# A language-model layer on one core: the state-space kernel for four channels per partition, with longer rows and weight columns further apart

## The reference, cut to what matters

```
h  = adaptive embedding(ids) * 16                    # gather of 384 values, times a 384 x 256 matrix
xn = layernorm(h)
x1 = xn @ w1.T + b                                   # 256 channels
xc = silu(depthwise conv of x1, 3 taps)
y[b, t, c] = D[c] * xc[b, t, c] + sum over u <= t of  K[c, t - u] * xc[b, u, c]
             with K[c, n] = sum over 16 states s of B[c, s] * C[c, s] * sigmoid(A[c, s]) ** n
h  = h + (y * silu(xn @ v1.T + b)) @ w2.T + b
h  = h + (shared gated MLP + mean of 2 hashed experts)(layernorm(h)) / 2
```

## Time and profile before

| | us |
|---|---|
| median of three runs | 439.96 |
| the profiled execution, its time | 440.18 |
| its span, first to last instruction | 438.3 |
| phase A, until the first matmul with Toeplitz weights | 130.2 |
| state-space matmuls | 130.2 to 157.6 |
| first expert matmul | 175.5 |

### The profile page before, as it was taken

One profiled execution on the slowest core, in us unless ns is written; L12 is line 12 of the kernel. 1 busy time (PEld: TensorE's weight loads), 2 busy tenths in 40 slices (PEclk: granted clock), 3 DMA queues, 4 the chain that ended last, 5 costly groups with the idle time before them and its releaser, 6 DMA issues.

```text
span 438.3 us, 8454 instructions
## 1 busy us (share of the span) xinstructions
PE 399.5 (91%) x2880; PEld 351.6 (80%) x2880; DVE 272.8 (62%) x607; ACT 243.5 (56%) x435; POOL 211.5 (48%) x236
## 2 busy tenths in 40 slices
PE   3869999899998874999999999999999999998996
PEld 2858788788677863788898988988988888897885
DVE  6667998889756778464565565564554654655333
ACT  4567777768887436635535635635635536435442
POOL 6578988831005555648337247247247336433000
PEclk9999999999999989899999999999999999999999
DMA  2424111249699982101111211201301301100101
GB/s 63 145 80 161 49 58 57 65 129 323 182 312 303 239 314 96 50 0 49 53 45 48 59 40 49 84 11 48 96 0 49 96 0 49 48 0 0 49 0 48
DMA packets 32779, 38.86 MB, mean 89 GB/s; under 512 B 3461, under 2 KB 29027, under 8 KB 32624
## 3 DMA queue, kind: packets, MB, share of 16 engines
q1 hardware_dynamic: 29616, 32.99, 24.3%
q0 software_dynamic: 3136, 5.52, 4.1%
HBM read 34.56 MB, written 8.65 MB: 99 GB/s over the span
## 4 chain that ended last, share of the span: by engine, by line
PE 65%; DVE 15%; POOL 6%; ACT 6%; issue 4%; DMA 3%; DVEq 0%; SPq 0%; ACTq 0%; POOLq 0%
PE ps L1152 20%; PE ps L1153 20%; PE ps L1154 20%; DVE hid_lo L1085 3%; DMA h_in<-h_rows_dram 2%; DVE stat L963 2%; POOL bias_e L657 1%; POOL bias_e L658 1%; PE ps L1160 1%; PE ps L1271 1%; PE ps L1190 1%; DVE x_mid L1016 1%; DVE act_out L1079 1%; ACT act_out L857 1%; DVE catT_lo L956 1%
## 5 line engine op out<-in xcount | busy, mean ns | idle before, releaser
L1085 DVE SCALAR_TENSOR_TENSOR hid_lo<-act_out,hid_hi 128x512 fp32r<-128x512 f32 x64 | 54.4, 851 | 57.6 <-ACT hid_hi L870 57.6
L857 ACT ACTIVATE act_out<-ps,vec 128x512 f32<-128x512 f32 x32 | 22.0, 689 | 90.5 <-PE ps L1154 90.5
L1079 DVE SCALAR_TENSOR_TENSOR act_out<-ps,vec,act_out 128x512 f32<-128x512 f32 x32 | 24.0, 751 | 55.6 <-ACT act_out L857 55.6
L687 POOL TENSOR_TENSOR h_sb<-h_sb,bias_e 128x256 f32<-128x256 f32 x32 | 24.5, 769 | 53.6 <-DVE h2n L976 53.6
L1154 PE MATMUL ps<-h2nT_hi,sw_lo 128*128 128x512 f32 x128 | 50.0, 391 | 0.0
L1153 PE MATMUL ps<-h2nT_lo,sw_hi 128*128 128x512 f32 x128 | 50.0, 391 | 0.0
L1152 PE MATMUL ps<-h2nT_hi,sw_hi 128*128 128x512 f32 x128 | 49.9, 390 | 0.0
L680 POOL TENSOR_TENSOR zc_lo<-v_sb,zc_hi 128x256 fp32r<-128x256 f32 x32 | 28.9, 907 | 34.4 <-ACT zc_hi L847 34.4
L861 ACT ACTIVATE act_out<-ps,vec 128x512 f32<-128x512 f32 x32 | 22.1, 689 | 40.4 <-PE ps L1154 40.3
L537 POOL DMA_INDIRECT cat<-table_dram,x_ids x32 | 35.7, 1115 | 8.4 <-issue 5.8
L870 ACT ACTIVATE hid_hi<-act_out 128x512 fp32r<-128x512 f32 x64 | 39.7, 622 | 0.0
(11 more groups left out here) (133 smaller groups left out, 1254.2 us busy)
## 6 DMA issues: line engine op xcount, KB each, us to landing
toep_l<-kernel_rows_dram SPq DMA_DIRECT2D x14, 512.0 KB, 9.0
toep_r<-kernel_rows_dram SPq DMA_DIRECT2D x12, 512.0 KB, 6.4
h_rows_dram<-h_ring SPq DMA_DIRECT2D x32, 128.0 KB, 1.8
h_in<-h_rows_dram SPq DMA_DIRECT2D x8, 512.0 KB, 4.5
stage<-w_e_dram POOLq DMA_DIRECT2D x7, 512.0 KB, 3.6
out_dram<-o_sb SPq DMA_DIRECT2D x7, 512.0 KB, 3.2
bias_e<-rows_dram SPq DMA_DIRECT2D x1, 1024.0 KB, 7.3
toep_r<-kernel_rows_dram SPq DMA_DIRECT2D x4, 256.0 KB, 7.7
```

The costliest lines, as they stand in the source:

```text
L687: nc.gpsimd.tensor_tensor(at, at, bias_e[:, bass.ds(e, 1), :].rearrange("p o c -> p (o c)"), ALU.add).then_inc(h2_biased, 1)
L857: nc.scalar.activation(act_out[:, n % 4, :], ps[bank][:, :], ACT.Silu, bias=vec[:, C_SB1 + j:C_SB1 + j + 1]).then_inc(act_done, 1)
L1079: nc.vector.scalar_tensor_tensor(act_out[:, n % 4, :], ps[bank + 1][:, :], vec[:, C_SB3 + j:C_SB3 + j + 1], act_out[:, n % 4, :], ALU.add, ...
L1085: nc.vector.scalar_tensor_tensor(hid_lo[:, n % 4, :], act_out[:, n % 4, :], 0.5 if kind == SHARED else 0.25, f32(hid_hi[:, n % 4, :]), ALU ...
```

## The change: what it does

- Rows in DRAM are for four channels: 16 bytes per position. A Toeplitz tile is [128, 4 groups, 128 lags, 4 channels, high/low], so its runs are 2 KB (1 KB in the half parts that were 512 bytes) and there are half as many. The same weights lie 8 f16 apart instead of 4, 16 bytes.
- Each partition computes K for four channels (64 states) and 64 lags: partitions 0 to 63 lags 0 to 63, partitions 64 to 127 lags 64 to 127, whose first value is multiplied with the decay to the power 64. The parameters come by two loads of their own (`k_par`), issued ahead of the weights; `vec` is loaded after them.
- DVE squares six times, forms the first values (two linked products) and doubles up to 16 lags per state, the last on 1024 elements after the fourth embedding split; the two products for `mid_bias` move there. POOL does one doubling in 8 steps, then 14 fold steps and the last sum, the D, the split: 26 steps instead of 30. The row is stored by two DMAs.
- The zeros in front of each row are copied once from the zeroed `x_pad` to DRAM by SP, and the memset of `k_row` goes. ACT waits for that copy before phase A, which writes `x_pad`.

```diff
-    toep_r = sb(ssm_mem, "toep_r", [P, TRIGHT, PAIRS, SEQ, 2, 2], F16, R)
+    toep_r = sb(ssm_mem, "toep_r", [P, TRIGHT, QUADS, SEQ, WIDE, 2], F16, R)
...
-    power = flat[:, 0:HALVES * STATES * SEQ].rearrange("p (s t) -> p s t", t=SEQ)
+    power = flat[:, 0:WIDE * STATES * HALF].rearrange("p (s t) -> p s t", t=HALF)
...
@@ SP
         sp.dma_start(x_ids[:, :, :], ids.rearrange("(g p r) -> p g r", p=P, r=RES)).then_inc(ids_in, 16)
+        for h in range(2):
+            params = bass.AP(small.tensor, C_A, [[2 * NSMALL, NQUAD], [NSMALL, 2], [1, NK]])
+            sp.dma_start(k_par[h * NQUAD:(h + 1) * NQUAD, :, :], params).then_inc(k_par_in, 16)
+        sp.dma_start(raw_a[:, 0:KC * D], w_a[:, 0:KC * D]).then_inc(wa_in, 16)
         sp.dma_start(vec[:, :], small).then_inc(vec_in, 16)
-        sp.dma_start(raw_a[:, 0:KC * D], w_a[:, 0:KC * D]).then_inc(wa_in, 16)
+        sp.wait_ge(pad_zero, 1)
+        sp.dma_start(bass.AP(kernel_rows.tensor, 0, [[YLEN * WIDE, NQUAD], [1, (SEQ - 1) * WIDE]]),
+                     x_pad[0:NQUAD, :, :, :].rearrange("p a b t -> p (a b t)")[:, 0:(SEQ - 1) * WIDE]).then_inc(rows_zero, 16)
...
-            src = bass.AP(kernel_rows.tensor, q * PAIRS * 2 * YLEN + 2 * (h * HALF + t),
-                          [[2, HALF], [2 * YLEN, PAIRS], [1, 2 * (SEQ - t)]])
+            src = bass.AP(kernel_rows.tensor, q * QUADS * WIDE * YLEN + WIDE * (h * HALF + t),
+                          [[WIDE, HALF], [WIDE * YLEN, QUADS], [1, WIDE * (SEQ - t)]])
...
@@ POOL, kernel_step
-            if n < 4:
+            if n < 8:
                 double(5, 8 * n, 8)
-            elif n < 12:
-                double(6, 4 * (n - 4), 4)
+            elif n < 16:
+                c, part = (n - 8) // 2, (n - 8) % 2
+                fold((slice(c, c + 1), slice(4 * part, 4 * part + 4)), 8)
...
+                for h in range(2):
+                    lags = bass.AP(kernel_rows.tensor, (SEQ - 1 + h * HALF) * WIDE, [[YLEN * WIDE, NQUAD], [1, HALF * WIDE]])
+                    row = k_row[h * NQUAD:(h + 1) * NQUAD, :, :, :].rearrange("p t c w -> p (t c w)").bitcast(F32)
+                    pool.dma_start(lags, row).then_inc(k_out, 16)
...
@@ DVE
-        double(0)
-        double(1)
+        for k in range(6):
+            square(k)
+        first = power[:, :, 0].rearrange("p (i s) -> p i s", i=2)
+        link(nc.vector.tensor_tensor(first, k_par[:, :, K_B:K_C], k_par[:, :, K_C:K_D], ALU.mult))
+        later = power[NQUAD:P, :, 0]
+        link(nc.vector.tensor_tensor(later, later, abar[NQUAD:P, 6, :], ALU.mult))
...
-        beside_cat = {0: lambda: double(2), 1: lambda: double(3), 2: lambda: double(4), 3: last_square}
+        beside_cat = {0: two_doubles, 1: lambda: double(2), 2: lambda: double(3), 3: last_double}
...
@@ PE
-                t_hi, t_lo = toep(q)[:, j // 2, :, j % 2, 0], toep(q)[:, j // 2, :, j % 2, 1]
+                t_hi, t_lo = [toep(q)[:, j // WIDE, :, j % WIDE, w] for w in range(2)]
```

More of the change, by code:

```diff
@@ L44 @@
 YLEN = 256
-PAIRS = CH // 2
+WIDE = 4
+QUADS = CH // WIDE
+NQUAD = D // WIDE
 HALF = SEQ // 2
 C_W1B, C_V1B, C_CONV = 0, 2, 4
-C_A, C_B, C_C, C_D = 10, 42, 74, 106
+C_A = 10
+K_A, K_B, K_C, K_D, NK = 0, 32, 64, 96, 98
 C_SB1, C_SB3, C_B1 = 108, 112, 116
@@ L564, in double, with fold @@
             k_link(nc.gpsimd.tensor_tensor(power[:, at, n:2 * n], power[:, at, 0:n], by, ALU.mult))
[L566 to L570, removed]
+        by_channel = power[:, :, :].rearrange("p (c s) t -> p c s t", c=WIDE)
+        def fold(at, keep):
+            by_s = by_channel[:, at[0], :, :]
+            first = by_s[:, :, at[1], :]
+            second = by_s[:, :, at[1].start + keep:at[1].stop + keep, :]
+            k_link(nc.gpsimd.tensor_tensor(first, first, second, ALU.add))
+        K_STEPS = 26
         def kernel_step(n):
-            halves = power[:, :, :].rearrange("p (h s) t -> p h s t", h=HALVES)
-            row_hi, row_lo = [k_row[:, SEQ - 1:2 * SEQ - 1, :, w].rearrange("p t c -> p c t") for w in range(2)]
+            row_hi, row_lo = [k_row[:, :, :, w].rearrange("p t c -> p c t") for w in range(2)]
+            if n >= K_STEPS:
+                return
             if n == 0:
@@ L579, in kernel_step @@
                 pool.wait_ge(k_pool, k_steps)
-            if n < 4:
+            if n < 8:
                 double(5, 8 * n, 8)
-            elif n < 12:
-                double(6, 4 * (n - 4), 4)
+            elif n < 16:
+                c, part = (n - 8) // 2, (n - 8) % 2
+                fold((slice(c, c + 1), slice(4 * part, 4 * part + 4)), 8)
             elif n < 20:
[L585 to L595, removed]
+                fold((slice(n - 16, n - 15), slice(0, 4)), 4)
+            elif n < 22:
+                fold((slice(2 * (n - 20), 2 * (n - 20) + 2), slice(0, 2)), 2)
+            elif n == 22:
+                k_link(nc.gpsimd.tensor_tensor(k_sum[:, :, :], by_channel[:, :, 0, :], by_channel[:, :, 1, :], ALU.add))
+            elif n == 23:
+                first = k_sum[0:NQUAD, :, 0].rearrange("p (i c) -> p i c", i=2)
+                k_link(nc.gpsimd.tensor_tensor(first, first, k_par[0:NQUAD, :, K_D:NK], ALU.add))
+            elif n == 24:
                 k_link(nc.gpsimd.tensor_copy(row_hi, k_sum[:, :, :]))
@@ L753, in _ @@
     def _(act):
-        act.wait_ge(vec_in, 16)
-        nc.scalar.activation(abar[:, 0, :], vec[:, C_A:C_A + 32], ACT.Sigmoid).then_inc(abar_done, 1)
+        act.wait_ge(k_par_in, 32)
+        nc.scalar.activation(abar[:, 0, :].rearrange("p (i s) -> p i s", i=2), k_par[:, :, K_A:K_B], ACT.Sigmoid).then_inc(abar_done, 1)
         act.wait_ge(half_set, 1)
@@ L921, in _ @@
         nc.vector.scalar_tensor_tensor(all_mask, all_ids, 0.0, all_mask, ALU.is_ge, ALU.mult).then_inc(mask_step, 1)
[L922 to L927, removed]
         dve.wait_ge(abar_done, 1)
@@ L936, in double @@
             n = 1 << k
-            by = abar[:, k, :].rearrange("p (s o) -> p s o", o=1).broadcast_to([P, HALVES * STATES, n])
+            by = abar[:, k, :].rearrange("p (s o) -> p s o", o=1).broadcast_to([P, WIDE * STATES, n])
             link(nc.vector.tensor_tensor(power[:, :, n:2 * n], power[:, :, 0:n], by, ALU.mult))
+        for k in range(6):
             square(k)
-        def last_square():
-            square(5)
-            assert steps == K_FIRST
-        double(0)
-        double(1)
+        first = power[:, :, 0].rearrange("p (i s) -> p i s", i=2)
+        link(nc.vector.tensor_tensor(first, k_par[:, :, K_B:K_C], k_par[:, :, K_C:K_D], ALU.mult))
+        later = power[NQUAD:P, :, 0]
+        link(nc.vector.tensor_tensor(later, later, abar[NQUAD:P, 6, :], ALU.mult))
         dve.wait_ge(wa_hi, 1)
@@ L950, in _, with two_doubles, last_double @@
                                 f32(proj_hi[:, :, :].rearrange("p k n -> p (k n)")), ALU.subtract).then_inc(wa_lo, 1)
-        beside_cat = {0: lambda: double(2), 1: lambda: double(3), 2: lambda: double(4), 3: last_square}
+        def two_doubles():
+            double(0)
+            double(1)
+        def last_double():
+            dve.wait_ge(vec_in, 16)
+            for half in range(HALVES):
+                nc.vector.tensor_tensor(mid_bias[:, half:half + 1], vec[:, C_W1B + half:C_W1B + half + 1],
+                                        vec[:, C_CONV + 3 * half + 1:C_CONV + 3 * half + 2], ALU.mult)
+            double(4)
+            assert steps == K_FIRST
+        beside_cat = {0: two_doubles, 1: lambda: double(2), 2: lambda: double(3), 3: last_double}
         def cat_lo(i, r):
```

25 lines of the change are left out of this document (13 added, 12 removed).

## The result

The changed kernel took 449.43 us (median of four runs, 448.91 to 450.69); the kernel before, on the same chip, 439.95 (four runs, 439.21 to 440.4). The ratio is 1.0217, 95% interval 1.0199 to 1.0235: 2.2% slower. The forecast was 449.7. The profiled execution took 449.91 us with a span of 448.0, 9.7 more than before.

The account below looks back on a forecast made before the run. PE, busy 91%, bounds the kernel, except where it waits for the first mixer output, set by POOL's chain. Weight step 8.7 plus late start 1.0 on 440.18 us gave 449.9, 0.2 less for timed runs: 449.7; range 438.3 to 451.3.

Parts of the forecast that it names:

- The weight step: State-space matmuls: weights 16 bytes apart double spacing from 33.3 to 66.7 ns; first mixer output 8.7 us later.
- the loads stay at full pace: Rival for state-space matmuls: weight loads do not feel the 16-byte step; 439.0 us; chance 0.40.
- a part of the price: Rival for state-space matmuls: spacing only 50 to 62 ns; at 60 ns, 446.3 us; chance 0.10.
- The turns between the tiles: PE's seven output turns between Toeplitz tiles, four transposes each, at 0.47 us: 3.3 us of the stage.
- The late start: Kernel's front: moved DVE doubling steps delay the first normalization and ACT's hn by 1.0 us (0 to 1.4).
- The idle time that I counted against it: DVE before L963 at 16.33 us: 0.4 us idle, to absorb part of the 1.2 us of added doubling work.
- parts 3 and 4: DVE's moved doubling steps (+1.0 us, early squares 0); POOL's reduced work, zeroing copy and extra parameter load and store (0).
- part 2: Toeplitz loads at 116 to 158 us: longer runs gain 0 to 5 us, taken as 2, worth nothing if weights slow.
- POOL's chain: Before the first mixer output: bias row, second h_in, expert weight splits, zc_lo; last before, no longer last after the change.
- 1.77 us of room: At the first mixer output: the PE chain ended 1.77 us before POOL's, so that much matmul delay costs nothing.
- a plain shift: From first mixer output to first expert matmul and the end: the same steps run, so output delay passes on unchanged.
- the first rival: Weight loads keep full pace despite 16-byte steps: 439.0 us, 435.3 at best; chance 0.40.

Follow-up runs that it names:

- experiment 1: Standalone kernel of equal matmuls, only the byte step between weight columns varied: f16 spacing 25.2 ns at 4 bytes, 33.7 at 8, 60.5 at 16.
- after_8B: Changed kernel with PE alone changed back to read weights 8 bytes apart: 443.17 us, ratio 1.0062 to the kernel before.
- before_16B: Kernel before with PE alone changed, reading Toeplitz weights 16 bytes apart: 447.23 us, ratio 1.0129 to the kernel before.
- after_rows_4352: Changed kernel, weights still 16 bytes apart, with DRAM rows 4352 bytes apart instead of 4096: 448.82 us, ratio 1.0199 to the kernel before.
- after_parts_of_double: Changed kernel with DVE's 1024-element doubling cut in four, after the fourth to seventh embedding splits: 449.18 us, ratio 1.0182 to the kernel before.
- before_rows_2304: Kernel before with rows of K in DRAM 2304 bytes apart instead of 2048: 437.20 us, ratio 0.9915 to the kernel before.
- Experiments 5: Changed kernel with weights read 8 bytes apart and DRAM rows 4352 bytes apart instead of 4096: 439.37 us, ratio 0.9962 to the kernel before.
- experiment 4: Standalone kernel only loading 8 x 512 KB in ten shapes, each twice: both passes 32.41 us as before the change, 33.27 as after.
- experiment 6: Changed kernel, weights 16 bytes apart, with DRAM rows 4352 bytes apart instead of 4096 (the run after_rows_4352): 448.82 us, ratio 1.0199.

## Why the prediction came out right

**The weight step, predicted 66.7 ns, measured 60.8.** The mechanism is shown, by experiments 1 and 2 and by `after_8B`. Doubling was too much because the 33.3 ns of before are not all reads: at 2 and 4 bytes the spacing is 25.2 and doesn't move, so something else sets it there. The rule of the Trainium skill ("SBUF — State Buffer", Door 1: two or more hits in a 16-byte line for full bandwidth) led the right way; the runs show no edge: two hits (8 bytes) cost 33.7 against 25.2 already, and 12 and 14 bytes lie between. Of the rivals, "the loads stay at full pace" fell. With it fell my reading of the Trainium skill, "TensorE: Matmul & The Clock Gate", Weight-path perf modes, by which a step up to 1,024 elements keeps the fast load: it says what may be loaded that way, not what it costs. The rival "a part of the price", at 60 ns, had the spacing right, and the time wrong by 3.1 us.

**The turns between the tiles, predicted 7 x 0.47 us.** This term failed. At 60 ns a matmul the granted clock fell to 0.5 at 137.7 us and stayed there for 27.3 us. PE had no gap in the stage before the fall, and only that of 0.24 us behind it. The f16 matmuls kept their spacing, as in experiment 1, but six of the seven turns took about 0.9: 6 x (0.9 - 0.47) = 2.6 us more. The stage by the measured terms: 512 x 0.060 = 30.7, the x turn 0.5, turns 6 x 0.9 + 0.5 = 5.9, one wait 0.4: 37.5, as measured. My terms gave 34.1 + 0.5 + 3.3 = 37.9. So the stage was right to 0.4 us because an error of 3.4 us met one of 2.6 with the opposite sign and a wait of 0.4 that was not counted. That is luck. The 2.6 us belong to this one execution, too: the stretch at half clock in the stage is 27.3 us here, and 20.5, 17.1 and 13.6 us in the three other profiled kernels with weights 16 bytes apart (`before_16B`, `after_rows_4352`, `after_parts_of_double`).

**The late start, predicted +1.0, measured +1.5 in the profiled pair.** The doubling took 1.22 us (predicted 1.21). The idle time that I counted against it was not a property of the kernel: `before_rows_2304`, whose start is that of before, has none there, and its first hn is at 16.25 where the profiled one of before has 17.05. Over seven profiled executions of before and its variants the first hn lies at 16.48 on average, over four of the changed kernel and its variants (without `after_parts_of_double`) at 18.23: 1.75. That is more than the doubling, because the front is late ahead of it, which parts 3 and 4 had at nothing. The first embedding split starts at 8.14 to 8.35 in the seven and at 8.83 to 9.13 in the four, and 0.57 us of that are left at the third one. PE's first turn waits for the gathered rows there (7.32 us, 6.83 before); why these land later was not tried. From the first hn to the first Toeplitz matmul it is 113.1 to 113.2 us in all seven, 113.5 to 113.9 in the four. So the start costs 2.2 us on average, most of the 0.6% of experiment 3. Experiments 5 and 8 agree: with faster loads and weights 8 bytes apart in both kernels, 0.9962 - 0.9915 = 0.47% is left, 2.1 us. That `after_parts_of_double` took 114.6 for this path shows that the doubling isn't all of it; where the last half microsecond goes in phase A stays open.

**The loads, predicted 0 to 5 us of gain, taken as 2.** There was no gain: 305 GB/s against 312. The ratio of 1.13 for longer runs, argued from one other load, is what experiment 4 finds for the run length alone (13% less time); what part 2 left out is that the rows also came to lie 4096 bytes apart, which costs more than that. The miss cost nothing, since PE's chain was last by then, as the prediction said it would be, and experiment 6 shows it: 373 GB/s give almost nothing while PE is the bound.

**What is late.** As forecast, POOL's chain is no longer last and its 1.77 us of room are used up. DVE needed 176.26 - 169.21 = 7.05 us behind the last matmul, against 7.65 before, so the output came 0.5 us earlier than the forecast shift. Between it and the first expert matmul it was 9.05 us, and 8.48 before, where the prediction had a plain shift: that gives the 0.5 us back. Behind that all moved together: from the first expert matmul to the end of the span it is 262.8 us, and 262.9 before.

**Two bounds of the prediction are added wrongly.** By its own terms, a spacing of 62 ns and nothing from part 3 give 439.96 + 8.1 - 1.8 = 446.3 us and not 447.5 (130.2 + 31.7 + 0.5 + 3.3 is 8.1 behind 157.6), and the first rival's best is 439.96 - 5 + 0.1 = 435.1 and not 435.3. No conclusion hangs on either.

## What to carry to other kernels

Count the bytes that a weight load walks over, not only its columns: 128 f16 weights at 16 bytes cost 60 ns, at 4 bytes 25, and a matmul of 32 or 64 columns hides none of it. A layout that makes DMA runs longer may place the weights further apart, and what is off the critical path gives nothing back. Longer runs and the distance of the rows are two things: change one at a time, and try the distance first. 256 more bytes gave 0.85% here with one constant changed. And a stretch of fixed times compares two kernels only where what it measures starts at the same time in both.

## What the runs showed of the hardware

- The price of a strided weight load (experiment 1) grows by 0.42 ns for each 16-byte line from 8 to 16 bytes (33.7, 47.0, 53.7, 60.5 ns) and lies at 57.2 to 62.3 from 24 to 64 bytes. With fp32r weights under 256 columns it is 119.9 ns up to 8 bytes and 231.6 at 16. At 2 and 4 bytes 25.2 ns is the floor. The Trainium skill, "TensorE: Matmul & The Clock Gate", section "Wait — 56ns, not 53.3ns?", names about 25 ns as the least from start to start, and the trace agrees.
- TensorE's clock fell to half while PE was busy for all of the time, once its matmuls came 60 ns apart: in the kernel from 137.7 us, in `weight_steps` between 534 and 540 us. At 33 ns apart it stayed at full for 640 matmuls without a gap. In the kernels with weights 8 bytes apart, where PE has waits in the stage, it fell too, for about 3 us within the stage, in seven of eight profiled executions (in `after_8B` at 147 to 151 us). The weight loads did not slow down with it; the f32 turns did, from 0.47 to 0.9 us.
- Overlapping reads of DRAM rows that lie 4096 bytes apart ran at 248 and 256 GB/s, at 4352 at 303 and 314 (4.19 MB in the times of experiment 4), and at 4096 with the partitions 256 bytes apart at 299. In the kernel before, 2304 bytes in place of 2048 meant 333 in place of 312 GB/s; in the changed one, 4352 in place of 4096 meant 373 in place of 305. The mechanism was not tried.
- DVE stands still beside a long POOL addition on SBUF (2.44 us for 0.40). The Trainium skill, "SBUF — State Buffer", Terms, describes a port pair that these two engines share and for which the loser waits; these rows agree.
